# The first expert stage reads rows that the first attention's tails have written in expert order, per turn

## What is computed

```python
x = x + xattn_0(ctx, layernorm(x), W0, W1)        # two hops of attention over ctx
# layer 0's experts: 8 experts, hidden width 512, the two best of each row
h      = layernorm(x)
logits = h @ router_w.T
vals, idx = top_k(logits, 2)
mix    = softmax(vals)
out    = (gelu(h @ w1.T + b1) @ w2.T + b2)[idx]   # of the two chosen experts
x      = x + sum(out * mix)
x = x + xattn_1(layernorm(x), ctx, Wq, bq, ...)   # a linear attention, 16 heads
```

## Time and profile of the kernel before

| | us |
|---|---|
| median of 3 runs | 1901.37 |
| lowest and highest | 1900.53, 1907.52 |
| the profiled execution's own time | 1909.33 |
| its span, first to last instruction | 1907.6 |

### The profile page before, as it was taken

The page is one execution under the profiler, slowest core; times in us unless marked ns, Lnnn a source line. Parts: engine busy times, 40 slices in busy tenths (PEclk is TensorE's granted clock), DMA queues, the critical chain, the costliest instruction groups (busy, mean ns, idle before and its releaser), DMA issues. The chain is left out here.

```text
span 1907.6 us, 36653 instructions
## 1 busy us (share of the span) xinstructions
PE 1488.1 (78%) x10440; PEld 1337.0 (70%) x10441; DVE 1164.3 (61%) x3672; ACT 824.9 (43%) x2537; POOL 763.8 (40%) x757
## 2 busy tenths in 40 slices
PE   6776999425677639999999999999994898446394
PEld 4555899313466539999999999999993787224294
DVE  4556344217867337787778777777775455574244
ACT  4343455201222126666666666666661232313152
POOL 2011543560000535454747474756454355011442
PEclk8786899756666769999999999999997899766597
DMA  9002322110011230000000000000001522200223
GB/s 190 1 0 70 118 65 59 47 48 1 1 45 45 57 97 13 1 12 1 24 1 22 0 22 1 21 0 11 3 10 34 149 72 65 89 9 14 63 64 114
DMA packets 91845, 79.06 MB, mean 41 GB/s; under 512 B 16820, under 2 KB 78871, under 8 KB 91623
## 3 DMA queue, kind: packets, MB, share of 16 engines
q1 hardware_dynamic: 70712, 44.92, 9.0%
q0 software_dynamic: 11936, 24.52, 4.4%
q10 hardware_dynamic: 9104, 8.53, 1.5%
HBM read 51.36 MB, written 27.60 MB: 41 GB/s over the span
## 5 line engine op out<-in xcount | busy, mean ns | idle before, releaser
L1838 POOL TENSOR_TENSOR paired_rows<-paired_rows,rinv 128x1024 f32<-128x1024 f32 x128 | 242.3, 1893 | 284.6 <-DVE rinv L2123 281.6
L2002 ACT ACTIVATE paired_rows<-psum_banks,neg_max 128x256 f32<-128x256 f32 x512 | 237.4, 490 | 0.2
L2114 DVE TENSOR_TENSOR probs_turned_lo<-psum_banks,probs_turned_hi 128x512 fp32r<-128x512 f32 x256 | 175.5, 686 | 96.4 <-ACT probs_turned_hi L1984 82.8
L1888 PE MATMUL psum_banks<-y_turned_parts,queries_hi 128*128 128x256 f32 x1024 | 199.9, 293 | 3.0 <-DVEq L1739 3.0
L1923 PE MATMUL psum_banks<-probs_turned_hi,y_rows 128*128 128x512 f32 x512 | 192.0, 416 | 0.4 <-issue 0.4
L1984 ACT CAST probs_turned_hi<-psum_banks 128x512 fp32r<-128x512 f32 x256 | 151.1, 590 | 57.5 <-PE psum_banks L1872 55.1
L1872 PE MATMUL psum_banks<-ident,paired_rows 128*128 128x128 f32 x1024 | 154.9, 274 | 7.8 <-DVEq L1739 4.4
L1888 PEld LDWEIGHTS psum_banks<-y_turned_parts,queries_hi 128*128 128x128 f32 x1024 | 158.0, 191 | 3.5 <-issue 3.5
L2128 DVE TENSOR_REDUCE neg_max<-psum_banks 128x4 f32<-128x1024 f32 x128 | 155.9, 1218 | 6.5 <-PE psum_banks L1888 3.5
L1984 ACT CAST queries_hi<-psum_banks 128x512 fp32r<-128x512 f32 x128 | 75.0, 586 | 172.5 <-PE psum_banks L1911 167.6
L1888 PE MATMUL psum_banks<-y_turned_parts,queries_lo 128*128 128x256 f32 x512 | 144.5, 282 | 0.0
(11 more groups left out here) (717 smaller groups left out, 3386.2 us busy)
## 6 DMA issues: line engine op xcount, KB each, us to landing
tile_rows__<-rows_by_expert SPq DMA_DIRECT2D x71, 64.5 KB
expert_rows<-expert_rows_sb SPq DMA_DIRECT2D x71, 64.0 KB, 1.5
normed_rows_dram<-paired_rows SPq DMA_DIRECT2D x2, 2048.0 KB, 8.9
staged_pairs<-expert_rows SPq DMA_DIRECT2D x8, 512.0 KB
paired_rows<-expert_rows SPq DMA_DIRECT2D x8, 512.0 KB, 6.0
tile_rows___<-rows_by_expert SPq DMA_DIRECT2D x39, 64.5 KB
x_rows<-in_x_dram SPq DMA_DIRECT2D x8, 256.0 KB, 5.3
expert_w_b<-in_L_ffn_w_dram SPq DMA_DIRECT2D x1, 2048.0 KB
```

What stands on the lines that cost most here:

```text
L1838: ins = pool.tensor_tensor(probs[:, p, :, :], probs[:, p, :, :], rinv[:, p, :].unsqueeze(2).to_broadcast([P, 4, 256]), ALU.mult)
L1888: ins = pe.matmul(bank[S_BANKS[par] + h // 2][:, (h % 2) * 256:(h % 2 + 1) * 256], queries[q][:, h, :], yparts[:, 2 * s2 + y, :], start=(k ...
L2002: ins = act.activation(probs[:, par, h, :], bank[S_BANKS[par] + h // 2][:, (h % 2) * 256:(h % 2 + 1) * 256], ACT.Exp, bias=nmax[:, par, h: ...
L2114: ins = dve.tensor_tensor(lo, bank[bank_][:, :], hi.bitcast(F32), ALU.subtract)
```

## The change

Layer 0's experts get the kept form, split by turn. In attention_0 the tails write each normalized row beside its pair number (129 wide, `ROWS` in `paired_rows`). At the end of a turn PE counts that turn's choices with four multiplications, DVE copies the counts (`counted`), and computes the places of the turn's 2 x 16 x 128 pairs (`places`): for the first turn this comes after the second turn's head norms, for the second at the stage's end. POOL writes the rows by indirect DMA to `rows_by_expert_and_turn`, one DMA for a tile and choice: 32 a turn. Before the second choice it overwrites the pair numbers with odd ones (L667), which waits until the first choice's rows have landed. 40 of the 64 DMAs are issued in attention_0. The other 24 go into experts(0)'s POOL program: 7 at its start, and one behind each of the first 17 output scatters.

Each turn has its own region for each expert, so there are up to 39 tiles for a turn and 78 in all (`TILES_FIRST`) instead of 71. SP fills the tiles' ends with pads, 8 a turn. The pads are made once, by POOL early in attention_0, for the later layers too, so that experts(1) no longer makes and stores them. The turning of the experts' weights moves from route(0) to the end of attention_0. `tile_tables` and the mixing weights are computed there too, and `route(0)` and its 2 MB store are gone. In experts(0) SP loads the tiles, POOL scatters the outputs to pair order, and attention_1 loads pairs on SP (`load_pairs`) in place of POOL's 64 fetches.

```diff
-SCATTERED = (1, 2, 3)
-KEPT = (2, 3)
+SCATTERED = (0, 1, 2, 3)
+KEPT = (0, 2, 3)
 REGION = B * P + P
+TURN_REGION = B * P // 2 + P
...
+TILES_TURN = (B * P + E * (P - 1)) // P
+TILES_FIRST = 2 * TILES_TURN
+TURN_TILES = E * TURN_REGION // P + E - 1
...
+            sp.wait_ge(pads_made.sem, 1)
+            as_tiles = lambda rows: rows.rearrange("(t p) d -> p t d", p=P)
+            sp.dma_start(as_tiles(pads_dram), pad_tiles[:, 0:2 * E, :]).then_inc(pads_stored.sem, 16)
+            sp.dma_start(as_tiles(xb[E * REGION:, :]), pad_tiles[:, 2 * E:2 * E + SPARE_TILES, :]).then_inc(pads_stored.sem, 16)
+            for i in range(TURNS):
+                at = (i * TURN_TILES + E * TURN_REGION // P) * P
+                mine = 2 * E + i * SPARE_TILES
+                sp.dma_start(as_tiles(xturn[at:at + SPARE_TILES * P, :]), pad_tiles[:, mine:mine + SPARE_TILES, :]).then_inc(pads_stored.sem, 16)
...
+        def kept_and_placed(pool, SS, i):
+            for w in range(W):
+                pool.wait_ge(SS[w].act.sem, SS[w].ACT.at(i, "tail_kept"))
+            pool.wait_ge(first_positions.sem, i + 1)
+
+        def spread_row(pool, i, k, t):
+            pool.indirect_dma_start(xturn, bass.IndirectOffsetOnAxis(ap=first_spots[:, i, k, t:t + 1], axis=0), ROWS[:, i * N + t, :], None).then_inc(first_rows_spread[2 * t // N].sem, 16)
+
+        def spread_first(pool, i, k, half):
+            for t in range(half * N // 2, (half + 1) * N // 2):
+                spread_row(pool, i, k, t)
+
...
+        def second_choice(pool, i, half):
+            pool.wait_ge(first_rows_spread[half].sem, (2 * i + 1) * 8 * N)
+            at = slice(i * N + half * N // 2, i * N + (half + 1) * N // 2)
+            pool.tensor_copy(ROWS.bitcast(U32)[:, at, P], odd_number[:, at])
+            pool.drain()
...
+        def late_spread(pool):
+
+            for t in range(N // 2, N):
+                spread_row(pool, TURNS - 1, 0, t)
+                yield
+            for half in range(2):
+                second_choice(pool, TURNS - 1, half)
+                for t in range(half * N // 2, (half + 1) * N // 2):
+                    spread_row(pool, TURNS - 1, 1, t)
+                    yield
 
...
+                    for i in range(TURNS):
+                        sp.wait_ge(first_ends.sem, i + 1)
+                        for e in range(E):
+                            at_ = sp.value_load(first_pad_at[0:1, i * E + e:i * E + e + 1], min_val=0, max_val=2 * TURN_TILES * P - P)
+                            n = (i * E + e) * P
+                            sp.dma_start(xturn[bass.ds(at_, P), :], pads_dram[n:n + P, :]).then_inc(first_pads.sem, 16)
...
+                    kept_and_placed(pool, SS, 0)
+                    spread_first(pool, 0, 0, 0)
                     weave(body(w, TURNS - 1, SS[w], T[w], False) for w in range(W))
+                    spread_first(pool, 0, 0, 1)
+                    for half in range(2):
+                        second_choice(pool, 0, half)
+                        spread_first(pool, 0, 1, half)
+                    kept_and_placed(pool, SS, 1)
+                    spread_first(pool, 1, 0, 0)
...
+                        for w in range(W):
+                            pe.wait_ge(SS[w].dve.sem, SS[w].DVE.at(i, "logits_kept"))
+                        for half, lhs in enumerate((tri, ones)):
+                            for k in range(2):
+                                ins = pe.matmul(T[0]["B"][:, half * N * E:(half + 1) * N * E], lhs[:, :], hot[:, k, :, :].rearrange("p t e -> p (t e)"), start=(k == 0), stop=(k == 1))
+                        ins.then_inc(first_places.sem, 1)
+                        pe.wait_ge(first_places_read.sem, i + 1)
+                    pe.wait_ge(weights_b.sem, weights_b.value)
+                    pe.wait_ge(loaded.sem, loaded.value)
...
+                        ins.then_inc(banks_turned.sem, 1)
...
+                    def counted(i):
+                        dve.wait_ge(first_places.sem, i + 1)
+                        dve.tensor_copy(begin[:, 0, :], region[:, i, :])
+                        dve.tensor_copy(got[:, :, :].rearrange("p a c -> p (a c)"), T[0]["B"][:, 0:2 * N * E]).then_inc(first_places_read.sem, 1)
+                        ch.link()
+
+                    def places(i):
+                        within, total = (got[:, a, :].rearrange("p (t e) -> p t e", e=E) for a in range(2))
+                        for e in range(E):
+                            dve.tensor_tensor_scan(upto[:, :, e], total[:, :, e], begin[:, :, e], 0.0, ALU.add, ALU.add)
+                        ch.link()
+                        dve.tensor_copy(first_pad_at[:, i * E:(i + 1) * E], upto[0:1, N - 1, :]).then_inc(first_ends.sem, 1)
+                        dve.tensor_copy(ends0[:, i, :], upto[:, N - 1, :])
+                        ch.link(dve.tensor_tensor(place[:, :, :], upto[:, :, :], total, ALU.subtract))
+                        ch.link(dve.tensor_tensor(place[:, :, :], place[:, :, :], within, ALU.add))
+                        ch.link(dve.tensor_tensor(picked[:, :, :, :], hot[:, :, :, :], place[:, :, :].unsqueeze(1).to_broadcast([P, 2, N, E]), ALU.mult))
+                        ch.link(dve.tensor_reduce(spot_f[:, :, :], picked[:, :, :, :], AX.X, ALU.add))
+                        dve.tensor_copy(first_spots[:, i, :, :], spot_f[:, :, :]).then_inc(first_positions.sem, 1)
                     for _ in next_rows(dve, ch, 0, st, here, (W,)):
...
+                            places(i - 1)
...
-                        weave(tail_dve(dve, ch, i * W + w, i, SS[w], T[w]["tl"], T[w]["A"]) for w in range(W))
+                        weave(tail_dve(dve, ch, i * W + w, i, SS[w], T[w]["tl"], T[w]["A"], [hot[:, 0, :, :], hot[:, 1, :, :]]) for w in range(W))
+                        counted(i)
+                    places(TURNS - 1)
+                    dve.tensor_tensor(leads[:, 0, :], MX[:, :, 1], MX[:, :, 0], ALU.subtract).then_inc(first_leads.sem, 1)
+                    for i in range(TURNS):
+                        tile_tables(dve, ch, TILES_TURN, ends0[:, i, :], region[:, i, :], marks, scratch, TURN_REGION, i * TURN_TILES, i * TILES_TURN)
+                        ch.link()
+                    dve.wait_ge(first_leads_exp.sem, 1)
+                    ch.link(dve.tensor_scalar(leads[:, 0, :], leads[:, 1, :], 1.0, None, ALU.add))
+                    ch.link(dve.reciprocal(WT[:, 0, :], leads[:, 0, :]))
+                    dve.tensor_tensor(WT[:, 1, :], WT[:, 0, :], leads[:, 1, :], ALU.mult)
                 close_streams(SS, ctx=True)
...
-            n_tiles = {0: TILES_TOP2, 1: TILES_CAP, 2: TILES_TOP2, 3: TILES_TOP1}[layer]
+            n_tiles = {0: TILES_FIRST, 1: TILES_CAP, 2: TILES_TOP2, 3: TILES_TOP1}[layer]
...
-                    if fixed:
-                        sp.wait_ge(pads_made.sem, 1)
-                        sp.dma_start(pads_dram.rearrange("(t p) d -> p t d", p=P), pads[:, 0:E, :]).then_inc(pads_stored.sem, 16)
-                        sp.dma_start(xb[E * REGION:, :].rearrange("(t p) d -> p t d", p=P), pads[:, E:E + SPARE_TILES, :]).then_inc(pads_stored.sem, 16)
-                        sp.wait_ge(pads_stored.sem, 32)
...
+                    def turn_is_here(i):
+                        for c in first_rows_spread:
+                            sp.wait_ge(c.sem, (i + 1) * 16 * N)
+                    if layer == 0:
+                        sp.wait_ge(first_pads.sem, 16 * TURNS * E)
+                        turn_is_here(0)
...
-                        with sp.Fori(1, n_tiles // SLOTS) as q:
-                            for u in range(SLOTS):
-                                load_tile(q * SLOTS + u, u)
+                        loops = [(1, n_tiles // SLOTS)]
+                        if layer == 0:
+                            loops = [(1, TILES_TURN // SLOTS), (TILES_TURN // SLOTS + 1, n_tiles // SLOTS)]
+                        for turn, (begin_, end_) in enumerate(loops):
+                            if turn:
+                                for j in range(loops[0][1] * SLOTS, begin_ * SLOTS):
+                                    if j == TILES_TURN:
+                                        turn_is_here(1)
+                                    load_tile(j, j % SLOTS)
+                            with sp.Fori(begin_, end_) as q:
+                                for u in range(SLOTS):
+                                    load_tile(q * SLOTS + u, u)
...
+                    late = late_spread(pool) if layer == 0 else iter(())
+                    for _ in range(LAST_ROWS_AHEAD):
+                        next(late, None)
...
+                            next(late, None)
...
-                @block.gpsimd
-                def _(pool):
-                    gather_turns(pool, layer_before)
-
                 @block.sync
                 def _(sp):
+                    load_pairs(sp, layer_before)
                     sp.wait_ge(SS[W - 1].dve.sem, SS[W - 1].DVE.at(TURNS - 1, "u_normed"))
...
-        route(0, 2, 0)
```

186 lines of the change are left out of this document (109 added, 77 removed).

## The result

The change makes the kernel 0.6% faster on the chip of the first comparison: 1894.0 us against 1902.43 us (medians of six runs each), a ratio of 0.9938 [0.9917, 0.996]. The profiled execution of after took 1896.3 us, its span is 1894.4 us and its mean granted clock 0.865. Forecast were 1862 us, in a range up to 1893: the sign is right, and the gain is a fifth of the one forecast. Between the two profiled executions it is 13.0 us, between the medians 8.4: that of before lies 6.9 us above its median, that of after 2.3.

The account below looks back on a forecast made before the run. It saw DVE busiest in route(0), PE bounding experts(0), and 65.85 us of waits beside POOL's fetches in attention_1. Terms A to H summed to -39 us: 1870 us profiled, 1862 as a median, range 1838 to 1893.

Parts of the forecast that it names:

- A: End of attention_0 and route(0): the first tile is turned at 182.8 instead of 193.35, -10.5 us (-14 to -5).
- B: POOL's write series inside attention_0 holds other engines at attention_3's share: +7 us (0 to +25).
- C: experts(0): seven more tiles at 1.99 us each, +14 us.
- D: experts(0): the kept form's pace, 2.04 us a tile as in experts(3), +3.5 us.
- E: Head of experts(0): 24 late writes, 17 of them behind scatters, and a POOL stall, +9.5 us (+3 to +14).
- F: End of experts(0): the stage now ends when the scatters have landed, +4 us (+3.4 to +7).
- G: attention_1 without fetches: its three long waits go, -63 us (-68 to -50).
- H: experts(1) without pads: its second tile no longer waits behind the pads' 1 MB, -3.5 us (-5 to 0).
- Rival 1: Stalls move with POOL's series into attention_0 and experts(0), costing 33 and up to 33 more: 1921 us, chance 0.06.
- rival 2: Fetches are not the cause of attention_1's waits, which stay in part: 1894 us if half, 1925 if all; chance 0.08.
- Rival 3: POOL bounds the head of experts(0) and the series costs twice, B at 14, E at 25: 1885 us, chance 0.16.

Follow-up runs that it names:

- e3b: After plus 64 unread back-to-back indirect writes by POOL in attention_1, on a chip where before takes about 1900 us: 1965.48 us.
- e9: After with late writes thinned and the next stage's weights issued in three parts between tile loads, where before takes about 1900 us: 1892.83 us, ratio 0.990.
- e1: After with the next stage's 3 MB of weights issued by ACT instead of SP, where before takes about 1800 us: 1837.65 us, ratio 1.0189.
- c_after: After, unedited, on a chip where before takes about 1800 us: median 1830.29 us, ratio to before 1.0118.
- e7: After with 9 late writes ahead and one behind every second scatter, where before takes about 1800 us: 1820.81 us, ratio to before 1.008.
- e13: e9 plus POOL waiting in attention_0 after every fourth write until landed, where before takes about 1800 us: 1824.42 us, ratio 1.0124.
- c_before: The kernel before, unedited, on a chip where it takes about 1800 us: 1807.27 us.
- e10: Before with one POOL clear and drain behind each attention_1 fetch, on a chip where before takes about 1900 us: 1967.22 us, ratio 1.0292.

## Why the prediction was wrong, step by step

*A, the end of attention_0 and route(0): right.* Forecast -10.5 with the tiles turned at 182.8; on kind B, where B is absent, -9.9 and 182.98 (180.2 to 183.9 over six kernels with this code). On kind A the pads took 15.88 us instead of 9.30, and ACT waited for two late signals, which is part of what follows.

*B, POOL's series in attention_0: this step failed most.* I priced it by attention_3's share, 4.9 of 20.1 us, "since the instruction is of the same kind": +7. It measured 10.4 - (-9.9) = +20.3 on kind A: 15.9 in the tails (177.3 against 161.5) and about 4.4 behind them. In e3b and e9, with the same attention_0 in the other comparison of kind A, the first tile is turned at 199.1 and 201.3, which makes B 16 and 18. The instruction's kind was the wrong thing to go by: e3b shows writes to do just what fetches do. The share was of no use either. My reading is that a wait costs only where an engine comes to another's product while the series runs, and a second turn with four streams comes to many; no run varied that.

*C and D, tiles and pace: C right, D short.* The steady pace is (380.0 - 292.5) / 42 = 2.083 us, and over 77 steps 160.4 us, against 139.6 before: +20.8 for the two, forecast 17.5. I took 2.04 from experts(3) for D. Where the other 0.04 us come from wasn't tried.

*E, the head of experts(0): failed.* What is left is 184.3 - 160.4 = +23.9 on kind A (11.3 on kind B), forecast 9.5. On kind B it is the size that the upper part of my bounds had. On A the late signals come on top, 16.5 us idle in three waits ahead of the outputs, for 184.3 - 172.2 = 12.1 us more in the stretch. Wrong as an argument, on both kinds, was that the ninth tile's load behind the weights is free because "its slot is free only after the first scatter anyway": e1 took the weights away, and of the gap of 8.1 us 2.1 were left. Wrong in size was the stall behind the first odd numbers, priced at 1 or 2 us: 6.20 us in after, 7.27 in c_after and 6.78 in e7, but 2.2 us in e1, e9 and e13, where the 3 MB are not just issued. The weights made both.

*F, the end of experts(0): short.* 7.1 us for 4. ACT's first copy of the next stage is 404.77 - 395.0 = 9.8 us behind the last output, where it was 343.63 - 341.0 = 2.6; the scatters' landing that I took from experts(3) gave 6.35, to an issue on a queue and not to a copy of ACT. No run took the remaining 3 us apart.

*G, attention_1 without fetches: right on the chip it was forecast for.* -65.6 for -63. And e3b shows it for the reason named: these three waits belong to the series. On kind B there were no such waits to remove, +0.8. No trace I had could show that; all of it came from one kind of chip.

*H, experts(1) without pads: right.* Of the 4.69 us of the earlier trace rows DVE waits 0.90 at that tile now, and experts(1) takes 42.7 us from its first turned tile to its last output in place of 47.3. The last stretch of the table gave 8.7 us on kind A; what is beyond this was not taken apart.

**The rivals.** Rival 1, that the stalls move with the series, got 0.06 and turned out half true: 20.3 less the 0 of kind B in attention_0 and 12.1 in experts(0), 32 us of the 65.6 that left attention_1, came back. It doesn't cost 33 and 33, since the share isn't a constant of the series. Against rival 2 the prediction held that the long "remote" waits it had found all begin while POOL's series runs. The trace of before has one more, DVE's 5.98 us to 53.71, ahead of the first indirect DMA; so it is e3b that refutes rival 2 for attention_1, and not that argument. Rival 3 came nearest, 1885 us at 0.16. Its conditions hold in part: the wait behind the odd numbers was over 5 us once (6.20) and 2.61 the second time, and the weights held the outputs for about 6 us (8.1 less the 2.1 of e1), not 10. Its E of 25 is close to the measured 23.9, and its B of 14 is 6 short. That its sum comes so near is partly luck, since on kind A 12.1 us of E are late signals, which it didn't price. The range failed because I had split one mechanism over several cases. The late signals set B and a part of E, so they went up together, and C to F all missed on the same side: -39 + 13.9 (A, B) + 16.6 (C to E) + 3.1 (F) = -5.4 before what G and the end gave back (7.8). That sum belonged into the range. The last few microseconds are a matter of the measure: I moved the profiled execution's difference over to the medians unchanged, which are 4.6 us closer together.

**The rule of the Trainium skill.** The prediction weighed the Trainium skill's page "SBUF — State Buffer", section "SBUF: two separate sides", by which DVE and GpSimd exclude each other from a shared pair of ports for one instruction at most. Nothing here shows a port holding DVE: in c_before it is busy for 34.86 of 37 us beside 28.12 us of POOL's fetches, and on kind A what the rows show late are signals, also ACT's to PE. So the lock explains none of it. But the conclusion drawn from the rule, that the fetches don't explain the 65.85 us, is refuted by e3b.

## What to carry to other kernels

A wait that comes from a series of GpSimd DMAs goes where the series goes: before moving one, look what in its new place hands products from engine to engine step by step, and price all new places as one risk, not as several. Time both kernels on more than one chip before a gain of a per cent is believed; this change is 0.6% faster on one kind and 1.2% slower on the other. And where a queue gets tile loads, nothing of several MB belongs between the first slots' loads and the next ones, even if the slots look full: here it cost between 3.7 us (e13 against e7) and 7.2 us (e1 against c_after).

## What the runs showed of the hardware

- On chips of one kind, while POOL issued indirect DMAs every 1.25 us (0.94 to 0.96 us busy, 0.30 between), TensorE's results were read late by VectorE and ScalarE: up to 37.12 us idle, 36.7 of them with PE's product done. ScalarE's signals to VectorE and TensorE came late as well, by 1.9 us at 145.3 in after. On chips of the other kind the same kernel showed 0.45 us in that place. The whole kernel before takes 1902 to 1909 us on the one and 1800 to 1809 on the other. What differs in the chips, nothing here shows.
- A late signal doesn't need indirect DMAs: on both kinds the kernel before has DVE idle for 6 us (5.98 and 6.30) at 53.7 and 54.0 us, with TensorE's product done 3 us before, no indirect DMA in the kernel yet and the DMA engines at a share of 1.19 and 1.32 for 1 GB/s. The cause is open.
- The delays are repeatable: writes of other data brought them back with ends 53.6, 76.1 and 89.4 us from the first DMA, where the fetches had 53.4, 75.8 and 89.1. At 3.34 us between DMAs they were gone (e10).
- Eight pad stores on SP took 15.88 to 16.70 us on one kind (after, e3b, e9) and 9.30 to 9.47 us on the other.
- Where POOL waits for indirect DMAs' landing, overwrites their source and drains, the next write starts 2.2 to 2.8 us after the overwriting. It is 6.20, 6.78 and 7.27 us in the one place where SP had just issued 3 MB of loads (after, e7, c_after), and 2.2 us there when the 3 MB stood elsewhere (e1, e9, e13).
